# The first four output tiles, not two, in turns by halves of k, with their loads in that order

## The chip, the cores and the metric

One core of a Trainium2 chip runs the kernel. The metric is device time in microseconds (us): 407.63 is the median of three runs before the change (407.6 to 407.68).

## What is computed

Eight sequences of 256 tokens, 1024 wide. Each sequence is first multiplied by a 1024 x 1024 matrix that its expert number picks (`weight[itok]`). The result goes through a base matrix with bias and through a routed low-rank update, and is added to x:

```python
w = weight[adapter_ids]
xc = jnp.einsum('bsi,boi->bso', x, w)
...
logits = xf @ W_router.T
probs = jax.nn.softmax(logits, axis=-1)
topk_p, topk_i = jax.lax.top_k(probs, TOP_K)
...
h = jnp.einsum('nd,erd->ner', xf, A_stack) * combine[..., None]
lora_out = jnp.einsum('ner,eor->no', h, B_stack) * SCALING
out = x + xf @ W_base.T + b_base + lora_out
```

All is float32.

## The kernel before

TensorE works on operands that are split in a high part (a cast to the reduced type, ScalarE, L488 and L466) and a low part (raw minus high, VectorE, L660 and L539). A product is high x high + high x low + low x high.

The sequences go in two groups of four. For each sequence s, the first stage (`cond`) makes eight output tiles t of 128 x 256. One output tile needs one weight tile of 512 KB (w(s,t), all eight k blocks) and the sequence's x (two halves of 512 KB, four k blocks each). On TensorE it is eight wide matmuls (L801: weight high against x high and low, 512 columns), then eight narrow ones (L805: weight low against x high, 256 columns). Tile t uses PSUM bank t % 4. When a tile is done, ScalarE copies a half of the bank (L503), VectorE adds the other half to it (L686), ScalarE casts the sum (L508), VectorE subtracts (L691). TensorE may use a bank again when L686 is done (`xc_summed`). After the odd sequences the router (L844, L845) multiplies these sums: its first matmul waits until L691 has run for 15 of the 16 tiles, the last k block for the 16th. Then come the low-rank product and, after four sequences, the base matrix.

All loads of x and weights go through six raw slots of 512 KB and, but for the first x half, through SyncE's queue, in the order of `load_order`. Before a load SyncE waits until VectorE has subtracted what lay in the slot. The slot of the n-th load is n % 6, and the order of the start is the list `START`. Ahead of the first weight load of a sequence SyncE reads the expert number from memory (L357), after the wait for that load's slot.

The head is special, since nothing is there yet. The x half (0,0) is loaded in two pieces by ScalarE's queue (`ACT_MOVES`), and others in pieces by SyncE (`SP_MOVES`: tile, first and last k block). Casts and subtracts go by pieces too (`HI_PIECES`, `LO_PIECES`, in that order on ScalarE and VectorE). `START_STEPS` says in which order TensorE takes halves of output tiles: (0, 0, 4) is tile 0 with k blocks 0 to 3. The first two tiles are done so: first half of 0, first half of 1, second half of 0, second half of 1. Ahead of them run 24 matmuls on zeros (`WARM`). Below, W2a is the first half (k blocks 0 to 3) of weight tile 2 of the first sequence, W2b the second, x a and x b the halves of x.

Of the kernel before, what the change touches and what calls it, by code (L numbers as in the profile page):

```python
# [12 lines left out]
P = 128  # L13
SEQS, TOK, D = 8, 256, 1024
KT = D // P
HT = KT // 2
# [34 lines left out]
            ("A22b", R2, (1, 1)), ("A12b", R0, (0, 1))]  # L51


STARTS = 4
START = [("x", 0, 0), ("w", 0, 0), ("w", 0, 1), ("x", 0, 1), ("w", 0, 2), ("w", 0, 3)]
X0, W0, W1, X1 = range(STARTS)
ACT_MOVES = [(X0, 0, 2), (X0, 2, 4)]
SP_MOVES = [(W0, 0, 4), (W1, 0, 4), (X1, 0, 4), (W0, 4, 8), (W1, 4, 8)]
HI_PIECES = [(X0, 0, 2), (X0, 2, 4), (W0, 0, 2), (W0, 2, 4), (W1, 0, 4), (X1, 0, 2), (X1, 2, 4), (W0, 4, 8),
             (W1, 4, 8)]  # L60
LO_PIECES = [(X0, 0, 2), (X0, 2, 4), (W0, 0, 2), (W0, 2, 4), (W1, 0, 4), (X1, 0, 2), (X1, 2, 4), (W0, 4, 8),
             (W1, 4, 8)]

START_STEPS = [(0, 0, 4), (1, 0, 4), (0, 4, 8), (1, 4, 8)]
WARM, WARM_N = 24, 2 * P

RESIDENT = {(0, 5): [("a", 0, 0)], (2, 5): [("b", 0, 0)]}

# [50 lines left out]
def split_order():  # L119

    order = START[STARTS:]
    for g in range(GROUPS):
# [23 lines left out]
def load_order():  # L146

    out, n = [], 0
    for g in range(GROUPS):
        ring = list(START) if g == 0 else []  # L150
        for s in range(GSEQS * g, GSEQS * (g + 1)):
# [19 lines left out]
def piece_count(pieces, i, k):  # L171

    return next(n + 1 for n, (j, a, b) in enumerate(pieces) if j == i and a <= k < b)


def tile_steps(i):
    return KT if START[i][0] == "w" else HT

# [19 lines left out]
def build(nc, x, ids, w_cond, w_base, w_router, lora_a, lora_b, bias, consts, out):  # L198
    with ExitStack() as ctx:
# [3 lines left out]
        def psum(name):  # L203
            return ctx.enter_context(nc.psum_tensor(name, [P, 512], F32))

        def sem(name):
            return ctx.enter_context(nc.semaphore(name))
# [34 lines left out]
        bank_x = [psum(f"bank_x{m}") for m in range(HT)]  # L242
# [7 lines left out]
        raw_in = [sem(f"raw_in{i}") for i in range(RAW)]  # L250
        start_in = {(i, b): sem(f"start_in{i}_{b}") for i, a, b in ACT_MOVES + SP_MOVES if b < tile_steps(i)}
        warm_clear = sem("warm_clear")
# [54 lines left out]
        def split_dst(key, hl):  # L307
            kind, i, j = key
            if kind == "w":
                return wc_hl[:, slot_of(i, j), hl]  # L310
            if kind == "x":
                return x_hl[:, i % 2, HT * j:HT * (j + 1), hl, :]
            if kind == "S":
                return wc_hl[:, pair_of(i, j[0]) + j[1], hl]
            if kind == "T":
                return half(t_buffer(j[0]), j[1])[:, :, hl]
            if kind == "a":
                return a_hl[:, hl]
            return b_hl[:, hl, 0:KT] if kind == "b" else b_hl[:, hl, KT:]
# [12 lines left out]
        def piece(v, i, a, b):  # L332

            n = v.shape[1] // tile_steps(i)
            return v[:, a * n:b * n]

        def piece_in(i, b):
            return raw_in[i] if b == tile_steps(i) else start_in[i, b]

        def move_piece(issuer, i, a, b, src):  # L340
            issuer.dma_start(piece(raw[:, i], i, a, b), piece(src, i, a, b)).then_inc(piece_in(i, b), 16)  # L341

        def moved(i, k):

            return piece_in(i, next(b for j, a, b in ACT_MOVES + SP_MOVES if j == i and a <= k < b))

        @block.sync
        def _(sp):
            ids_of = {}

            def source(key):
                kind, i, j = key
                if kind == "x":
                    return x[i, j]
                if kind == "w":
                    if i not in ids_of:
                        ids_of[i] = nc.sync.value_load(ids[0:1, i:i + 1], min_val=0, max_val=w_cond.shape[0] - 1)  # L357
                    return w_cond[bass.ds(ids_of[i], 1), j, :, :].rearrange("a p n -> (a p) n")
                if kind in ("a", "b"):
                    return lora_a if kind == "a" else lora_b  # L360
                oh, ih = next(q for name, _, q in QUARTERS if name == kind)
                return w_base[oh, ih, :, j, :]

            def wait_free(key):
# [18 lines left out]
            for n, (key, slot) in enumerate(LOADS):
                if n >= STARTS:
                    if slot in in_slot:
# [57 lines left out]
        def _(act):  # L443
            def hi(key):
                kind, i, j = key
                if key in SUM:
                    act.wait_ge(summed, SUM[key])
                elif kind == "S":
                    name = {P1: "A11", P2: "A12", P4: "A22b"}[j[0]]
                    slot, landed = LANDED[name, i, j[1]]  # L450
                    act.wait_ge(raw_in[slot], landed)
                elif kind != "T":
                    slot, landed = LANDED[key]
                    act.wait_ge(raw_in[slot], landed)

                if kind == "S" and j[0] >= P5:
                    act.wait_ge(product_done, made(i, j[0] - 2, 2 * j[1] + 1))
                if kind == "T" and j[0] in (P6, P7, P4):
                    act.wait_ge(product_done, made(i, {P6: P1, P7: P2, P4: P5}[j[0]], HT - 1))
                if kind == "x" and i and i % GSEQS == 0:  # L460
                    act.wait_ge(product_done, made(i // GSEQS - 1, P6, HT - 1))
                if kind == "x" and i > GSEQS and i % GSEQS == 1:
                    act.wait_ge(product_done, made(i // GSEQS - 1, P7, HT - 1))
                if kind == "w" and i and i % GSEQS == 0 and j < 4:
                    act.wait_ge(product_done, made(i // GSEQS - 1, P4 if j < 2 else P3, 2 * (j % 2) + 1))
                nc.scalar.copy(split_dst(key, HI), split_src(key)).then_inc(hi_done, 1)  # L466
# [17 lines left out]
            for i, a, b in ACT_MOVES:  # L484
                move_piece(nc.scalar, i, a, b, x[START[i][1], START[i][2]])
            for i, a, b in HI_PIECES:
                act.wait_ge(moved(i, b - 1), 16)
                nc.scalar.copy(piece(split_dst(START[i], HI), i, a, b), piece(split_src(START[i]), i, a, b)) \  # L488
                    .then_inc(start_hi, 1)
            for key in START[STARTS:]:  # L490
                hi(key)
# [41 lines left out]
        def _(dve):  # L533
# [123 lines left out]

            for i, a, b in LO_PIECES:
                dve.wait_ge(start_hi, piece_count(HI_PIECES, i, b - 1))
                nc.vector.tensor_tensor(piece(split_dst(START[i], LO), i, a, b), piece(split_src(START[i]), i, a, b),  # L660
                                        piece(split_dst(START[i], HI), i, a, b).bitcast(F32), ALU.subtract) \
                    .then_inc(start_lo, 1)
            for key in START[STARTS:]:
                lo(key)
# [118 lines left out]
        def _(pe):  # L783
# [24 lines left out]
            def first_cond():  # L808

                for t, a, b in START_STEPS:  # L810
                    w, ps = (W0, W1)[t], bank_x[t]
                    for k in range(a, b):
                        pe.wait_ge(start_hi, piece_count(HI_PIECES, w, k))
                        pe.wait_ge(start_lo, piece_count(LO_PIECES, X0 if k < HT else X1, k % HT))
                        wide(ps, 0, t, k)
                    for k in range(a, b):
                        pe.wait_ge(start_lo, piece_count(LO_PIECES, w, k))
                        mm = narrow(ps, 0, t, k)
                    if b == KT:
                        mm.then_inc(cond_done, 1)  # L820
# [99 lines left out]
            for g in range(GROUPS):  # L920
                for s in range(GSEQS * g, GSEQS * (g + 1)):
                    for t in range(KT):
                        if s == 0 and t < 2:
                            if t == 0:
                                first_cond()
                            continue
                        cond(s, t)
                        if s % GSEQS == 2 and t == 1:
                            gate_to_rows(2 * g)
                    if s % 2:  # L930
                        router(s // 2)
                        lora_down(s // 2)
                second(g, P1)
                gate_to_rows(2 * g + 1)
                for j in (P2, P5, P6, P7, P4, P3):
                    second(g, j)
# [42 lines left out]
```

## Time and profile before

| | |
|---|---|
| median of three runs | 407.63 us |
| the profiled execution, its own time | 407.98 us |
| its span in the trace | 406.2 us |
| TensorE busy | 399.7 us (98%) |
| VectorE busy | 302.5 us (74%) |
| ScalarE busy | 186.3 us (46%) |
| HBM read | 64.10 MB |

The span is what the trace covers; the time of an execution has 1.8 us around it. A busy share near 100% says which engine the end depends on, not that each of its instructions is fast. All times below are us from the start of the span.

### The profile page before, as it was taken

How to read it: one execution, taken by the hardware profiler on the slowest of the kernel's cores; microseconds unless marked ns; L12 is line 12 of the kernel's file. 1: busy time of each engine (PE TensorE's matmuls, PEld its weight loads, DVE VectorE, ACT ScalarE, POOL GpSimd, SP SyncE). 2: the span in 40 equal slices, each digit the busy share in tenths (PEclk: the TensorE clock that was granted, in tenths of full speed). 3: DMA queues.
4: the chain of work that ended last, by engine and by line, in shares of the span. 5: the costliest groups of instructions: out<-in, count | busy, mean ns of one | idle time of the engine just before them, and what ended most of it. 6: DMA issues, size and time to landing. Idle time of an engine off the chain costs nothing.

```text
span 406.2 us, 5339 instructions
## 1 busy us (share of the span) xinstructions
PE 399.7 (98%) x2008; PEld 338.7 (83%) x2008; DVE 302.5 (74%) x432; ACT 186.3 (46%) x286; POOL 39.9 (10%) x67
## 2 busy tenths in 40 slices
PE   7999999999999999999999999999999999999996
PEld 6788888888888888888888888888888888888885
DVE  3888947789799999764547697478868999987322
ACT  4776834758633345221145686257666233441000
POOL 0101100101000130011162000000000003001110
PEclk9999999999999999999999999999999999999999
DMA  6999780778430056376569878146184003621222
GB/s 228 361 322 318 295 329 24 249 247 284 156 103 2 27 181 208 129 242 224 194 216 368 298 246 302 61 148 224 44 266 142 7 21 103 200 94 76 79 79 77
DMA packets 21210, 72.84 MB, mean 179 GB/s; under 512 B 2832, under 2 KB 2848, under 8 KB 21184
## 3 DMA queue, kind: packets, MB, share of 16 engines
q1 hardware_dynamic: 15984, 56.11, 40.1%
q0 software_dynamic: 4912, 15.87, 11.1%
q10 hardware_dynamic: 288, 0.52, 0.4%
q8 instruction: 16, 0.26, 0.3%
q14 instruction: 10, 0.08, 0.1%
HBM read 64.10 MB, written 8.39 MB: 178 GB/s over the span
## 4 chain that ended last, share of the span: by engine, by line
PE 96%; DMA 1%; SPq 1%; DVE 0%; issue 0%; ACT 0%
PE bank_x L801 29%; PE bank_x L805 15%; PE bank_y L786 9%; PE bank_y L787 9%; PE bank_y L788 9%; PE bank_x L786 8%; PE bank_x L787 8%; PE bank_x L788 8%; PE bank_y L844 2%; PE bank_y L845 2%; DMA raw<-w_cond 1%; PE bank_y L868 0%; SPq L357 0%; SPq L341 0%; PE bank_y L860 0%; DVE out_sb L590 0%
## 5 line engine op out<-in xcount | busy, mean ns | idle before, releaser
L801 PE MATMUL bank_x<-x_hl,wc_hl 128*128 128x512 f32 x512 | 128.8, 393 | 2.1 <-ACT wc_hl L488 2.1
L466 ACT CAST wc_hl<-raw 128x1024 fp32r<-128x1024 f32 x90 | 94.0, 1051 | 69.4 <-PE bank_y L788 34.8
L539 DVE TENSOR_TENSOR wc_hl<-raw,wc_hl 128x1024 fp32r<-128x1024 f32 x90 | 108.7, 1220 | 23.0 <-ACT wc_hl L466 22.9
L801 PEld LDWEIGHTS bank_x<-x_hl,wc_hl 128*128 128x128 f32 x512 | 92.1, 189 | 18.9 <-ACT wc_hl L488 2.5
L805 PEld LDWEIGHTS bank_x<-x_hl,wc_hl 128*128 128x128 f32 x512 | 70.1, 190 | 5.2
L805 PE MATMUL bank_x<-x_hl,wc_hl 128*128 128x256 f32 x512 | 71.7, 282 | 0.0
L582 DVE SCALAR_TENSOR_TENSOR out_sb<-bank_x,bias_sb,out_sb 128x512 f32<-128x512 f32 x32 | 23.7, 747 | 24.6 <-PE bank_x L788 19.1
L418 POOL DMA_DIRECT2D out<-out_sb x28 | 15.3, 545 | 257.7 <-DVE out_sb L590 236.1
L786 PE MATMUL bank_x<-x_hl,wc_hl 128*128 128x512 f32 x96 | 37.4, 389 | 0.0
L788 PE MATMUL bank_x<-x_hl,wc_hl 128*128 128x512 f32 x96 | 37.4, 389 | 0.0
L787 PE MATMUL bank_x<-x_hl,wc_hl 128*128 128x512 f32 x96 | 37.3, 389 | 0.0
L508 ACT CAST xc_hl<-xp 128x256 fp32r<-128x256 f32 x64 | 26.0, 406 | 24.0 <-DVE xp L686 23.8
L503 ACT COPY xc_low<-bank_x 128x256 f32<-128x256 f32 x64 | 23.7, 370 | 25.1 <-PE bank_x L805 24.9
L686 DVE TENSOR_TENSOR xp<-bank_x,xc_low 128x256 f32<-128x256 f32 x64 | 26.8, 418 | 7.7 <-ACT xc_low L503 7.4
L691 DVE TENSOR_TENSOR xc_hl<-xp,xc_hl 128x256 fp32r<-128x256 f32 x64 | 26.8, 419 | 7.6 <-ACT xc_hl L508 7.6
L590 DVE TENSOR_TENSOR out_sb<-bank_y,out_sb 128x512 f32<-128x512 f32 x24 | 16.4, 688 | 18.6 <-PE bank_y L788 17.8
L412 POOL DMA_DIRECT2D out_sb<-x x32 | 22.7, 714 | 76.2 <-PE bank_x L805 76.0
L786 PE MATMUL bank_y<-xc_hl,wc_hl 128*128 128x512 f32 x64 | 25.0, 390 | 0.0
L787 PE MATMUL bank_y<-xc_hl,wc_hl 128*128 128x512 f32 x64 | 24.9, 389 | 0.0
L788 PE MATMUL bank_y<-xc_hl,wc_hl 128*128 128x512 f32 x64 | 24.9, 389 | 0.0
L466 ACT CAST x_hl<-xp 128x1024 fp32r<-128x1024 f32 x16 | 16.6, 1051 | 13.8 <-DVE xp L543 13.5
L786 PEld LDWEIGHTS bank_x<-x_hl,wc_hl 128*128 128x128 f32 x96 | 18.0, 188 | 3.8
(94 smaller groups left out, 507.7 us busy)
## 6 DMA issues: line engine op xcount, KB each, us to landing
raw<-w_cond SPq DMA_DIRECT2D x62, 512.0 KB, 5.3
raw<-w_base SPq DMA_DIRECT2D x24, 512.0 KB, 5.0
out_sb<-x POOLq DMA_DIRECT2D x32, 256.0 KB, 5.5
raw<-x SPq DMA_DIRECT2D x15, 512.0 KB, 5.1
out<-out_sb POOLq DMA_DIRECT2D x28, 256.0 KB, 2.3
raw<-w_cond SPq DMA_DIRECT2D x4, 256.0 KB, 4.8
out<-out_sb SPq DMA_DIRECT2D x4, 256.0 KB, 2.0
raw<-x ACTq DMA_DIRECT2D x2, 256.0 KB, 2.8
```

The costliest lines, as they stand in the source:

```text
L466: nc.scalar.copy(split_dst(key, HI), split_src(key)).then_inc(hi_done, 1)
L503: nc.scalar.copy(xc_low[:, t % 2], bank_x[t % HT][:, TOK:]).then_inc(low_copied, 1)
L508: nc.scalar.copy(xc_hl[:, t, HI, s % 2 * TOK:(s % 2 + 1) * TOK], xp[:, s // 2 % 2, t, s % 2 * TOK:(s % 2 + 1) * TOK]).then_inc(xc_hi, 1)
L539: nc.vector.tensor_tensor(split_dst(key, LO), split_src(key), split_dst(key, HI).bitcast(F32), ALU.subtract).then_inc(lo_done, 1)
L582: nc.vector.scalar_tensor_tensor(out_sb[:, o], bank_x[m][:], bias_sb[:, i:i + 1], out_sb[:, o], ALU.add, ALU.add).then_inc(pass_done, 1)
L686: nc.vector.tensor_tensor(xc, bank_x[t % HT][:, 0:TOK], xc_low[:, t % 2], ALU.add) \
L691: nc.vector.tensor_tensor(xc_hl[:, t, LO, s % 2 * TOK:(s % 2 + 1) * TOK], xc, xc_hl[:, t, HI, s % 2 * TOK:(s % 2 + 1) * TOK].bitcast(F32), ...
L786: nc.tensor.matmul(ps, w_hi, v_hi, start=start, stop=False, skip_group_check=resumed)
L787: nc.tensor.matmul(ps, w_hi, v_lo, start=False, stop=False, skip_group_check=resumed)
L788: return nc.tensor.matmul(ps, w_lo, v_hi, start=False, stop=stop, skip_group_check=resumed)
L801: nc.tensor.matmul(ps[:], wc_hl[:, slot_of(s, t), HI, k], x_hl[:, s % 2, k].rearrange("p h n -> p (h n)"), start=(k == 0), stop=False)
L805: return nc.tensor.matmul(ps[:, TOK:], wc_hl[:, slot_of(s, t), LO, k], x_hl[:, s % 2, k, HI], start=False, stop=(k == KT - 1))
```

## The change

The first four output tiles are taken in turns: first halves of 0, 1, 2, 3, then second halves of 0, 1, 2, 3. The loads are put in the order of use: x a, W0a, W1a, W2a, x b, W3a, W0b, W1b, W2b, W3b. Formerly x b came after W1a, and W2 and W3 were each one load of 512 KB, behind W1b. W0a is loaded in two pieces of 128 KB. The places of x b and W2 in the six slots are exchanged. One warm matmul of 24 is left out.

```diff
-STARTS = 4
-START = [("x", 0, 0), ("w", 0, 0), ("w", 0, 1), ("x", 0, 1), ("w", 0, 2), ("w", 0, 3)]
-X0, W0, W1, X1 = range(STARTS)
+STARTS = 6
+START = [("x", 0, 0), ("w", 0, 0), ("w", 0, 1), ("w", 0, 2), ("x", 0, 1), ("w", 0, 3)]
+X0, W0, W1, W2, X1, W3 = range(STARTS)
 ACT_MOVES = [(X0, 0, 2), (X0, 2, 4)]
-SP_MOVES = [(W0, 0, 4), (W1, 0, 4), (X1, 0, 4), (W0, 4, 8), (W1, 4, 8)]
-HI_PIECES = [(X0, 0, 2), (X0, 2, 4), (W0, 0, 2), (W0, 2, 4), (W1, 0, 4), (X1, 0, 2), (X1, 2, 4), (W0, 4, 8),
-             (W1, 4, 8)]
...
+SP_MOVES = [(W0, 0, 2), (W0, 2, 4), (W1, 0, 4), (W2, 0, 4), (X1, 0, 4), (W3, 0, 4), (W0, 4, 8), (W1, 4, 8),
+            (W2, 4, 8), (W3, 4, 8)]
+HI_PIECES = [(X0, 0, 2), (X0, 2, 4), (W0, 0, 2), (W0, 2, 4), (W1, 0, 4), (W2, 0, 4), (X1, 0, 2), (X1, 2, 4),
+             (W3, 0, 4), (W0, 4, 8), (W1, 4, 8), (W2, 4, 8), (W3, 4, 8)]
+LO_PIECES = HI_PIECES
+
+START_STEPS = [(t, a, a + HT) for a in (0, HT) for t in range(4)]
+WARM, WARM_N = 23, 2 * P
...
-                    w, ps = (W0, W1)[t], bank_x[t]
+                    w, ps = (W0, W1, W2, W3)[t], bank_x[t]
...
-                        if s == 0 and t < 2:
+                        if s == 0 and t < 4:
```

On ScalarE, from its first casts of the start on (the names in brackets are semaphores: start_in1_2 is the load of the first two k blocks of start tile 1, raw_in4 the last load into slot 4):

```order
-L488 CAST wc_hl<-raw 128x256 [waits start_in1_4] x2
+L488 CAST wc_hl<-raw 128x256 [waits start_in1_2]
+L488 CAST wc_hl<-raw 128x256 [waits start_in1_4]
 L488 CAST wc_hl<-raw 128x512 [waits start_in2_4]
-L488 CAST x_hl<-raw 128x2x256 [waits raw_in3] x2
+L488 CAST wc_hl<-raw 128x512 [waits start_in3_4]
+L488 CAST x_hl<-raw 128x2x256 [waits raw_in4] x2
+L488 CAST wc_hl<-raw 128x512 [waits start_in5_4]
 L488 CAST wc_hl<-raw 128x512 [waits raw_in1]
 L488 CAST wc_hl<-raw 128x512 [waits raw_in2]
-L466 CAST wc_hl<-raw 128x1024 [waits raw_in4]
-L466 CAST wc_hl<-raw 128x1024 [waits raw_in5]
```

The cast of W2a now stands ahead of the two casts of x b and that of W3a right behind them; the whole tiles W2 and W3 are gone from behind W1b, and their second halves take their place.

On SyncE's queue, at the loads of the second half of the start (those on L341 wait for nothing, the next on L387 are the first that wait for a slot):

```order
 L341 DMA raw<-w_cond 128x512
-L387 ISA
-L387 DMA raw<-w_cond 128x1024
-L387 ISA
-L387 DMA raw<-w_cond 128x1024
+L341 ISA
+L341 DMA raw<-w_cond 128x512
+L341 ISA
+L341 DMA raw<-w_cond 128x512
+L341 ISA
+L341 DMA raw<-w_cond 128x512
 L387 ISA [waits start_lo]
 L387 DMA raw<-w_cond 128x1024
```

Two loads of whole weight tiles have become loads of halves, so ten loads, not seven, go out on SyncE before the first that waits for a slot.

## Rows read from the trace of the kernel before

**Rows 1.** Page: busy time per engine; granted clock in slices.

```profile
PE 399.7 (98%) x2008; PEld 338.7 (83%) x2008; DVE 302.5 (74%) x432; ACT 186.3 (46%) x286; POOL 39.9 (10%) x67
...
PEclk9999999999999999999999999999999999999999
```

**Rows 2.** Waits of TensorE, 0 to 110 us: total, times, longest.

```profile
PE bank_x L801 <- ACT wc_hl L488: 2.1, 2, 1.5
```

**Rows 3.** Timeline of TensorE: start us, duration us, what, [idle before].

```profile
6.50 1.19 PE L801 MATMUL bank_x<-x_hl,wc_hl 128*128 128x512 f32 x4 [0.56 <-ACT wc_hl L488]
...
11.06 1.19 PE L801 MATMUL bank_x<-x_hl,wc_hl 128*128 128x512 f32 x4 [1.50 <-ACT wc_hl L488]
...
12.57 1.09 PE L801 MATMUL bank_x<-x_hl,wc_hl 128*128 128x512 f32 x4
...
13.97 2.02 PE L801 MATMUL bank_x<-x_hl,wc_hl 128*128 128x512 f32 x8
...
19.57 0.63 PE L801 MATMUL bank_x<-x_hl,wc_hl 128*128 128x512 f32 x2
```

**Rows 4.** Timeline of ScalarE, 2 to 16 us.

```profile
6.05 0.71 ACT L488 CAST wc_hl<-raw 128x256 fp32r<-128x256 f32 x2 [1.35 <-DMA raw<-w_cond]
...
8.95 1.14 ACT L488 CAST x_hl<-raw 128x512 fp32r<-128x512 f32 x2 [1.35 <-DMA raw<-x]
10.39 0.62 ACT L488 CAST wc_hl<-raw 128x512 fp32r<-128x512 f32 x1 [0.31 <-DMA raw<-w_cond]
11.30 0.62 ACT L488 CAST wc_hl<-raw 128x512 fp32r<-128x512 f32 x1 [0.28 <-DMA raw<-w_cond]
12.78 1.05 ACT L466 CAST wc_hl<-raw 128x1024 fp32r<-128x1024 f32 x1 [0.86 <-DMA raw<-w_cond]
14.02 1.05 ACT L466 CAST wc_hl<-raw 128x1024 fp32r<-128x1024 f32 x1 [0.20 <-DMA raw<-w_cond]
```

**Rows 5.** All waits of ScalarE, 14.5 to 50.4 us.

```profile
ACT xc_hl L508 <- DVE xp L686: 5.0, 8, 1.4
ACT wc_hl L466 <- DMA raw<-w_cond: 2.4, 3, 1.5
ACT a_hl L466 <- DMA raw<-lora_a: 0.2, 1, 0.2
```

**Rows 6.** Timeline of all engines ahead of the router.

```profile
48.77 1.05 ACT L466 CAST wc_hl<-raw 128x1024 fp32r<-128x1024 f32 x1 [0.69 <-DMA raw<-w_cond]
...
50.50 0.37 ACT L503 COPY xc_low<-bank_x 128x256 f32<-128x256 f32 x1 [0.37 <-PE bank_x L805]
...
52.23 0.42 DVE L691 TENSOR_TENSOR xc_hl<-xp,xc_hl 128x256 fp32r<-128x256 f32 x1 [0.47 <-ACT xc_hl L508]
52.98 0.19 PEld L844 LDWEIGHTS bank_y<-xc_hl,wr_hl 128*128 128x128 f32 x1
```

**Rows 7.** Timeline of ScalarE near 28 us.

```profile
27.94 1.05 ACT L466 CAST wc_hl<-raw 128x1024 fp32r<-128x1024 f32 x1 [1.54 <-DMA raw<-w_cond]
```

**Rows 8.** Timeline of SyncE's queue: issues of loads.

```profile
2.79 0.94 SPq L341 DMA_DIRECT2D raw<-w_cond  x2
...
21.02 1.30 SPq L387 DMA_DIRECT2D raw<-w_cond  x2
```

**Rows 9.** Timeline of VectorE: subtract of weight tile 4, ahead of SyncE's expert read.

```profile
16.59 1.22 DVE L539 TENSOR_TENSOR wc_hl<-raw,wc_hl 128x1024 fp32r<-128x1024 f32 x1
```

**Rows 10.** Line L357, 0 to 60 us: ns min/median/max, first and last start.

```profile
L357 SPq TENSOR_LOAD <-ids_ptr x3: 837/1357/2169, 0.7 to 39.5; - x3
```

**Rows 11.** DMA in 2.4:3.2, in 4:6 and in 28:33 us.

```profile
DMA packets 161, 0.30 MB, mean 371 GB/s; under 512 B 16, under 2 KB 16, under 8 KB 161
...
DMA packets 257, 0.49 MB, mean 243 GB/s; under 512 B 25, under 2 KB 25, under 8 KB 257
...
DMA packets 559, 2.03 MB, mean 406 GB/s; under 512 B 64, under 2 KB 64, under 8 KB 559
```

**Rows 12.** Windows: length, busy per engine, clock, DMA share, GB/s.

```profile
21.50:22.00 0.50, 0.50 (x6) 0.50 (x5) 0.50 (x1) 0.50 (x3) 0.00 (x0) 1.00 0.41 81
```

More of the change, by code:

```diff
@@ L51 @@
             ("A22b", R2, (1, 1)), ("A12b", R0, (0, 1))]
-STARTS = 4
-START = [("x", 0, 0), ("w", 0, 0), ("w", 0, 1), ("x", 0, 1), ("w", 0, 2), ("w", 0, 3)]
-X0, W0, W1, X1 = range(STARTS)
+STARTS = 6
+START = [("x", 0, 0), ("w", 0, 0), ("w", 0, 1), ("w", 0, 2), ("x", 0, 1), ("w", 0, 3)]
+X0, W0, W1, W2, X1, W3 = range(STARTS)
 ACT_MOVES = [(X0, 0, 2), (X0, 2, 4)]
-SP_MOVES = [(W0, 0, 4), (W1, 0, 4), (X1, 0, 4), (W0, 4, 8), (W1, 4, 8)]
-HI_PIECES = [(X0, 0, 2), (X0, 2, 4), (W0, 0, 2), (W0, 2, 4), (W1, 0, 4), (X1, 0, 2), (X1, 2, 4), (W0, 4, 8),
-             (W1, 4, 8)]
[L61 to L65, printed above, removed]
+SP_MOVES = [(W0, 0, 2), (W0, 2, 4), (W1, 0, 4), (W2, 0, 4), (X1, 0, 4), (W3, 0, 4), (W0, 4, 8), (W1, 4, 8),
[5 more added lines that the diff above has]
+WARM, WARM_N = 23, 2 * P
 RESIDENT = {(0, 5): [("a", 0, 0)], (2, 5): [("b", 0, 0)]}
```

## The prediction

> **What bounds the kernel now.** I read the page's first lines, then the chain of waits, then the timelines of the first 20 us, then everything up to 56 us on the engines that feed TensorE. TensorE is busy for 399.7 of 406.2 us at granted clock 1.00 in all stretches read [rows 1], so the end moves only if TensorE idles less. Up to 110 us TensorE waits for data in two places, 2.1 us together, both for a cast of ScalarE on line L488 [rows 2]. The timeline of TensorE shows them [rows 3]: 0.56 us before the first product at 6.50, and 1.50 us before 11.06. A half-step (four wide and four narrow matmuls of one output tile) takes 12.57 - 11.06 = 1.51 us right after a stall and 13.97 - 12.57 = 1.40 us else. From 11.06 six half-steps' worth follow without a gap, until output tile 4 starts at 19.57, 8.51 us later.
>
> Why does it stall at 11.06? ScalarE is itself idle, waiting for DMA, before almost every cast [rows 4]: the second half of x could be cast at 8.95, the second half of weight tile 0 (W0b below; a and b are halves of k) at 10.39. Its cast takes 0.62, and TensorE starts at 11.06. So the head of the kernel is bound by bytes arriving. The order of arrival, in KB summed from the first piece of x on, was: 1536 at 8.95, 1792 at 10.39, 2048 at 11.30, 2560 at 12.78, 3072 at 14.02.
>
> **A second bound, behind the first.** Between 14.5 and 50.4 us ScalarE never waits for TensorE: its waits are for VectorE and for DMA alone [rows 5]. It copies the banks and casts the next tiles late, always after TensorE has long finished. So in that stretch the chain SyncE -> DMA -> ScalarE -> VectorE runs in its own time and does not get faster when TensorE does. It meets TensorE again at the router: its first matmul (L844) starts its weight load at 52.98, and needs the low part of the 15th output tile, which VectorE ends at 52.23 + 0.42 = 52.65 [rows 6]. With 0.04 us for the hand-over (cast end 11.02 to start 11.06 in [rows 3, 4]) the slack is 52.98 - 52.69 = **0.29 us**. Backwards, that subtract stands on VectorE behind the subtract of a weight tile whose cast, at 48.77, ended an idle of 0.69 for a DMA [rows 6]. What set this chain's pace earlier is again a DMA: 1.54 us of idle before the cast at 27.94 [rows 7]. Those loads went out from SyncE at 21.02 and later [rows 8], after SyncE had waited for weight tile 4's low part (16.59 + 1.22 = 17.81, [rows 9]) and then read the second sequence's expert number; 21.02 - 17.81 = 3.2 us.
>
> **The change, part by part.**
>
> *One warm matmul less.* The warm matmuls are followed by an idle 0.56 [rows 3] and nothing waits for their end: 0. TensorE's clock is granted in full in every slice, the one with the 1.50 us stall too [rows 1], so I expect nothing from that side.
>
> *W0a in two loads of 128 KB.* The first cast now needs half the bytes. Before, 256 KB issued at 2.79 could be cast at 6.05. At the 371 GB/s that the x pieces reached [rows 11] 128 KB take 0.35, so the first product may start about 0.3 earlier. But this gains nothing at the end if TensorE stalls for bytes again afterwards, and it will (next item). Its cost: one more issue on SyncE ahead of all others. Two issues take 0.94 us [rows 8], so one half a microsecond, and the DMA engines were not full then: 243 GB/s between 4 and 6 us [rows 11]. Everything behind may come 0 to 0.5 us later; I take 0.15, near the low end: an issue takes half a microsecond while its 256 or 512 KB take 0.7 or 1.4 at 371 GB/s, so a backlog forms behind the first loads and a late issue vanishes in it.
>
> *Four tiles by halves, loads in that order.* TensorE now has three half-steps (W0a, W1a, W2a) on the first x half where it had two. The matmuls are the same in number and shape. W2a's 256 KB go ahead of the second x half, so that half lands 256 KB later. Now the fourth half-step, W3a. It needs W3a cast, and in ScalarE's order that stands behind the casts of x's second half. W3a is complete when 2048 KB are in, exactly the place of W1b before: 11.30. Plus cast 0.62, hand-over 0.04, and the 0.15 above: TensorE can start it at about 12.1. ScalarE is free by then (x's 512 KB, done at 1792 KB = 10.4, two casts 1.14, end 11.5). Meanwhile TensorE: the first two half-steps began at 6.50 and ended at 11.06 - 1.50 = 9.56 before; 0.3 earlier and with W2a's 1.40 behind them they end at 10.7: **it stalls for about 1.4 us again**, in place of 1.50. After it five half-steps remain to tile 4, not six: 8.51 - 1.40 = 7.11. Tile 4 starts at 12.1 + 7.11 = 19.2 instead of 19.57: **gain 0.36**, between 0.0 (all half a microsecond late) and 0.5 (nothing late). Each later half comes in time: W0b would be cast at 12.7 for 13.6, W1b at 13.5 for 15.0, W3b (3072 KB, 14.02) at 14.8 for 17.8. VectorE has halves to subtract where it had two whole tiles, and can begin each as soon as its cast is done, so W3b's low part should be there near 15.5.
>
> *Tile 4 and the slots.* Raw slots of W0 and W1 are freed later, by the later landing of W0b and W1b (1.3 us each: 512 KB of others now go first), so the loads of weight tiles 5 and 6 go out near 13.4 and 14.1. The DMA queue may run dry near 14.5 for half a microsecond. It ran dry at 21.5 anyway (81 GB/s [rows 12]), because SyncE sat in the expert read, so that is taken back before the loads at 21.02. Cost 0, and 0.5 if that cover fails. Weight tile 4 itself lands at the same sum of bytes. Its subtract can begin at 16.4 to 17.0 (before 16.59): the second chain moves by D = -0.2 to +0.4; I take 0.
>
> *Sum.* The router can start 0.29 - D earlier and TensorE arrives 0.36 earlier; the smaller counts. Gain 0.29. Against the profile's own time: 407.98 - 0.29 = 407.69; the median of the runs is 0.35 below that execution, so **407.3**. Behind the router TensorE bounds again (ScalarE waits for it from 50.5 on, [rows 6]), and the gain stays.
>
> **A rule against the change.** The smallest loads in sight, 2 KB rows, ran at 371 GB/s, the 4 KB rows at 406 [rows 11]. By these, the 1 MB of W2 and W3 that now goes in 2 KB rows costs 1049 / 371 - 1049 / 406 = 0.24 us more (1049 thousand bytes); that is inside D. By the row the time is 407.3 to 407.6. The Trainium skill ("DMA: Bandwidth & Descriptors", section "Bandwidth") asks to batch loads to 1 MiB or more for three quarters of the peak, and would count every cut as a loss; its section on small descriptors knows only about three cycles of overhead per packet, which is closer to this row. By the first of the two the time would be that of the second rival, by the other the forecast.
>
> **The rivals.**
> 1. *Forecast*: stall moved, not removed; router caps the gain. 407.1 to 407.6. Chance 0.60.
> 2. *Smaller loads slow the bytes.* W0b and W1b, 256 KB each, came 0.91 apart; W2 and W3, 512 KB each, 1.24 apart [rows 4]. If the size makes the difference, four halves take 3.64 where two whole tiles took 2.48: weight tile 4 is 1.16 later, the expert read and all behind it as well, D = 1.1, and TensorE waits 1.1 - 0.29 = 0.8 at the router: **408.4**. It ends slower than before as soon as D is above 0.29. For it: those intervals. Against: 371 GB/s in [rows 11]. (The Trainium skill's rule on batching, above, would lead here.) Chance 0.2, and most of it part-way, 407.7 to 408.4.
> 3. *The stall goes and the chain moves too.* If W3a arrived by 10.7, TensorE would gain 1.8; still 0.29 - D is the cap, so the chain must be faster. The expert's read could be: its first part took between 0.84 and 2.17 us in the three reads up to 60 us [rows 10]. With D = -0.4 to -0.8 the gain is 0.7 to 1.1, the time 406.5 to 406.9. Against: nothing makes the bytes come sooner. Chance 0.08.
> 4. *The change does nothing*: the earlier issues cost 0.5 and W3a starts at 12.45. 407.6 to 407.8. Chance 0.12.
>
> **How the numbers follow.** 407.3 is the first case. A measurement of this kernel can tell about 0.2%, 0.8 us. Faster by more needs case 3 at its end: 0.05. Slower by more needs case 2 at its full price or a little over: 0.06. The range 406.8 to 408.1 leaves out the far ends of cases 2 and 3, some 1 in 10.
>
> **What the changed profile would show.** Right: TensorE idle 1.2 to 1.5 us before a group near 12.1 with L488 as the releaser, tile 4 near 19.2, no ScalarE wait for TensorE until about 50, and a new small idle, or none, before L844 near 52.7. Wrong: a wait at the router of half a microsecond (case 2; the loads of the second sequence issued after 21.5), or no stall near 11 and the router at 51. The prediction breaks if a load behind slot order, such as tile 5's, comes after 20.9: TensorE wants it at 19.2 + 2.8 = 22.0, and its cast takes 1.05 [rows 4].

## The result and the profile after

The changed kernel takes 409.11 us (median of 14 runs) against 407.99 us of the kernel before beside it: ratio 1.0026, interval 1.0015 to 1.0038. It was measured three times in all, each time beside the kernel before; its median was 1.12, 0.69 and 0.38 us above that kernel's, on average **0.73 us** (resampled over all runs: 0.49 to 1.08). Forecast was 407.3, that is 0.3 faster than the 407.63 on record. Of the 1.8 us between 407.3 and 409.11, 0.36 is no effect of the change: the kernel before itself took 407.99 beside it, not 407.63. The single runs of this first measurement spread over 2 us, from 407.76 to 409.87. The profiled execution took 408.6 us. One slow execution of e2 below, at 1030 us, is left out of its median.

The page of the changed kernel, to be held against [rows 1]:

```profile
span 406.8 us, 5366 instructions
...
PE 400.5 (98%) x2007; PEld 339.1 (83%) x2007; DVE 302.8 (74%) x434; ACT 186.4 (46%) x288; POOL 40.0 (10%) x67
...
PEclk9999999999999999999999999999999999999999
```

TensorE is busy 0.8 us longer at the same clock, and the span is 0.6 longer. The timeline of TensorE at the head (columns as in [rows 3]):

```profile
6.24 1.08 PE L801 MATMUL bank_x<-x_hl,wc_hl 128*128 128x512 f32 x4
...
7.72 1.20 PE L801 MATMUL bank_x<-x_hl,wc_hl 128*128 128x512 f32 x4
...
9.69 1.19 PE L801 MATMUL bank_x<-x_hl,wc_hl 128*128 128x512 f32 x4 [0.31 <-ACT wc_hl L488]
...
11.98 1.18 PE L801 MATMUL bank_x<-x_hl,wc_hl 128*128 128x512 f32 x4 [0.64 <-ACT wc_hl L488]
...
19.08 2.00 PE L801 MATMUL bank_x<-x_hl,wc_hl 128*128 128x512 f32 x8
```

The first product starts at 6.24, 0.26 earlier; the cast of its two k blocks was done at 5.50 + 0.76 / 2 = 5.88 (the two casts at 5.50 took 0.76 us), and TensorE comes to it straight from the warm matmuls, without an idle. W3a starts at 11.98 after an idle of 0.64, and tile 4 at 19.08 instead of 19.57. So far this is the forecast (12.1 and 19.2); of the 1.4 us of stall that it foresaw, 0.64 stand before W3a and 0.31 before W2a, and the half-steps between took longer (9.69 - 7.72 - 0.31 = 1.66, 11.98 - 9.69 - 0.64 = 1.65). The loss comes at the end of the second sequence. Who TensorE waited for (whole execution; total, times, longest), to be held against [rows 2]:

```profile
PE bank_x L801 <- ACT wc_hl L488: 0.9, 2, 0.6
PE bank_y L844 <- DVE xc_hl L691: 0.9, 1, 0.9
```

```profile
53.08 0.43 DVE L691 TENSOR_TENSOR xc_hl<-xp,xc_hl 128x256 fp32r<-128x256 f32 x1 [0.47 <-ACT xc_hl L508]
53.62 0.19 PEld L844 LDWEIGHTS bank_y<-xc_hl,wr_hl 128*128 128x128 f32 x1 [1.07 <-issue]
53.65 0.47 PE L844 MATMUL bank_y<-xc_hl,wr_hl 128*128 128x512 f32 x1 [0.89 <-DVE xc_hl L691]
```

The low part of the 15th tile ends at 53.08 + 0.43 = 53.51, not at 52.65 as in [rows 6], and the router's first weight load goes at 53.62 instead of 52.98. That is +0.64, and the span grew by 406.8 - 406.2 = 0.6. In the profiles quoted here the span is this moment plus 353.2: 52.98 and 406.2 before, 53.62 and 406.8 after. So nothing behind the router changed the time.

Where does the second chain lose its time? The chain that ended last, in order of time (start, duration):

```profile
13.61 1.38 DVE wc_hl L660 x2
...
15.01 7.68 DMA raw<-x
...
22.72 1.06 ACT x_hl L466
...
23.80 1.23 DVE x_hl L539
...
53.08 0.44 DVE xc_hl L691
...
53.65 0.47 PE bank_y L844
```

Between 23.80 and 53.08 all of its pieces are VectorE's and ScalarE's. In this profile it hangs on the load of the second sequence's first x half: issued at 15.01, landed at 22.69. Before, it was issued at 13.18:

```profile
13.18 0.43 SPq L387 DMA_DIRECT2D raw<-x  x1
```

After, with the five last loads of the start (L341) first, and in the last row the first weight loads of the second sequence, which went out at 21.02 before [rows 8]:

```profile
5.46 2.81 SPq L341 DMA_DIRECT2D raw<-w_cond  x5
...
15.01 0.34 SPq L387 DMA_DIRECT2D raw<-x  x1
...
22.04 0.85 SPq L387 DMA_DIRECT2D raw<-w_cond  x2
```

ScalarE, after, shows the same (compare [rows 4]; the cast of that x half was at 20.18 before):

```profile
12.21 2.71 ACT L488 CAST wc_hl<-raw 128x512 fp32r<-128x512 f32 x4 [0.28 <-DMA raw<-w_cond]
...
18.30 1.05 ACT L466 CAST wc_hl<-raw 128x1024 fp32r<-128x1024 f32 x1 [1.13 <-DMA raw<-w_cond]
...
22.72 1.05 ACT L466 CAST x_hl<-raw 128x1024 fp32r<-128x1024 f32 x1 [1.52 <-DMA raw<-x]
```

It is idle for 1.13 and 1.52 us waiting for tile 5 and for that x half. What VectorE loses by it is in the windows (length, then busy time of PE, PEld, DVE, ACT and POOL with their counts, clock, DMA share, GB/s). Before:

```profile
8.00:10.00 2.00, 1.56 (x10) 1.18 (x8) 0.72 (x2) 1.05 (x2) 0.00 (x0) 1.00 0.95 308
10.00:12.00 2.00, 0.94 (x4) 0.80 (x5) 1.63 (x4) 1.32 (x3) 0.00 (x0) 1.00 1.02 400
...
14.00:23.00 9.00, 9.00 (x53) 7.91 (x52) 8.98 (x13) 8.15 (x13) 1.74 (x3) 1.00 0.90 332
23.00:32.00 9.00, 9.00 (x52) 7.87 (x52) 7.87 (x12) 5.83 (x10) 0.71 (x1) 1.00 0.98 353
32.00:37.00 5.00, 5.00 (x31) 4.45 (x30) 3.00 (x6) 3.40 (x8) 0.20 (x1) 1.00 0.96 333
```

After:

```profile
8.00:10.00 2.00, 1.69 (x9) 1.30 (x9) 0.73 (x2) 0.62 (x1) 0.00 (x0) 1.00 0.84 232
10.00:12.00 2.00, 1.36 (x9) 1.00 (x7) 1.43 (x3) 1.66 (x3) 0.00 (x0) 1.00 0.86 251
...
14.00:23.00 9.00, 9.00 (x52) 7.87 (x51) 6.95 (x11) 5.85 (x11) 1.75 (x3) 1.00 0.87 318
23.00:32.00 9.00, 9.00 (x52) 7.88 (x51) 8.20 (x12) 8.13 (x14) 0.71 (x1) 1.00 0.95 343
32.00:37.00 5.00, 5.00 (x31) 4.41 (x30) 3.53 (x7) 2.19 (x5) 0.70 (x1) 1.00 0.96 348
```

Two things are to be seen. VectorE was busy 8.98 of 9.00 us between 14 and 23, and is now for 6.95. Of the 2.03 us lost it has caught up 0.33 + 0.53 = 0.86 by 37. The rest is 1.17; at the router it is late by 0.86, so some 0.3 more were caught up behind 37. It could catch up because in the kernel before it had an idle of its own behind 23, for the cast of a weight tile of the second sequence:

```profile
29.02 1.23 DVE L539 TENSOR_TENSOR wc_hl<-raw,wc_hl 128x1024 fp32r<-128x1024 f32 x1 [1.07 <-ACT wc_hl L466]
```

And between 8 and 12 us the DMA engines moved 2 x (308 + 400) = 1416 KB before and 2 x (232 + 251) = 966 KB after. The change promised to use the bytes better; it gets fewer of them.

### The profile page after: what moved, and what is told of

It reads as the page before. It is cut to its first block, busy times and chain, and to the rows that moved or that the text cites. A ratio compares the mean times of both kernels' runs of the same rounds, so it can differ in the third digit from the quotient of the medians.

```text
span 406.8 us, 5366 instructions
## 1 busy us (share of the span) xinstructions
PE 400.5 (98%) x2007; PEld 339.1 (83%) x2007; DVE 302.8 (74%) x434; ACT 186.4 (46%) x288; POOL 40.0 (10%) x67
## 4 chain that ended last, share of the span: by engine, by line
PE 86%; DVE 7%; DMA 3%; SPq 1%; ACT 1%; issue 0%
PE bank_x L801 22%; PE bank_x L805 11%; PE bank_y L786 9%; PE bank_y L788 9%; PE bank_y L787 9%; PE bank_x L786 8%; PE bank_x L788 8%; PE bank_x L787 8%; DVE wc_hl L539 3%; DMA raw<-x 2%; PE bank_y L844 2%; PE bank_y L845 2%; DMA raw<-w_cond 2%; DVE x_hl L539 1%; DVE xp L686 1%; DVE xc_hl L691 1%
## 5 line engine op out<-in xcount | busy, mean ns | idle before, releaser
L466 ACT CAST wc_hl<-raw 128x1024 fp32r<-128x1024 f32 x88 | 91.9, 1051 | 67.8 <-PE bank_y L788 34.8
L539 DVE TENSOR_TENSOR wc_hl<-raw,wc_hl 128x1024 fp32r<-128x1024 f32 x88 | 106.4, 1221 | 22.2 <-ACT wc_hl L466 22.2
L590 DVE TENSOR_TENSOR out_sb<-bank_y,out_sb 128x512 f32<-128x512 f32 x24 | 16.4, 689 | 18.6 <-PE bank_y L788 17.8
```

Of the source, the lines that this page charges most:

```text
L539: nc.vector.tensor_tensor(split_dst(key, LO), split_src(key), split_dst(key, HI).bitcast(F32), ALU.subtract).then_inc(lo_done, 1)
```

## The experiments

All differences are to the kernel before measured beside it, median against median, in us. Single runs scatter by about 1 us either way, so one difference is good to 0.3 or 0.4; the profiles say more on the mechanism than the times.

**e1 and g3, the changed kernel again.**

> The changed kernel once more, unaltered, beside the others. About 1.0 us over the kernel before. The router's first matmul waits 0.5 to 1.2 us for VectorE; TensorE starts output tile 4 near 19.1.

> The changed kernel unaltered, a third time: 0.6 to 1.1 us over the kernel before; 240 to 260 GB/s between 10 and 12 us.

+0.69 (ratio 1.0015, 1.0003 to 1.0028) and +0.38 (1.0008, 0.9996 to 1.0020). Both are slower than the kernel before, as expected, but by less than the 1.0 and the 0.6 to 1.1 expected. In the three profiles (the result's, e1's, g3's) TensorE started tile 4 at 19.08, 19.58 and 19.40 and waited 0.9, 0.4 and 1.3 us for VectorE at the router. The x half of the next sequence was issued at 15.01, 15.73 and 15.77 and cast at 22.72, 21.98 and 23.51. So the wait is there each time. But the x half alone does not set its size: in e1 it was cast 0.74 us earlier than in the first profile, and VectorE was as late at the router (0.82 against 0.86 us). There another load held the chain behind it, that of the low-rank matrix, which SyncE issued at 23.92, right behind the second sequence's first two weight loads (23.02; 21.02 before):

```profile
30.42 1.05 ACT L466 CAST a_hl<-raw 128x1024 fp32r<-128x1024 f32 x1 [1.33 <-DMA raw<-lora_a]
```

These loads stand behind SyncE's read of the expert number. In the three profiles they went out at 22.04, 23.02 and 22.95. Tile 4's low part, for which the read waits, ended at 17.86, 18.56 and 18.57 (17.81 before), and from there to the issue it took 4.2, 4.5 and 4.4 us (3.2 before).

**e4, small loads alone.**

```diff
-SP_MOVES = [(W0, 0, 4), (W1, 0, 4), (X1, 0, 4), (W0, 4, 8), (W1, 4, 8)]
+SP_MOVES = [(W0, 0, 4), (W1, 0, 4), (X1, 0, 4), (W0, 4, 8), (W1, 4, 8), (W2, 0, 4), (W2, 4, 8), (W3, 0, 4),
+            (W3, 4, 8)]
...
+START_STEPS = [(0, 0, 4), (1, 0, 4), (0, 4, 8), (1, 4, 8), (2, 0, 8), (3, 0, 8)]
```

> The kernel before with W2 and W3 each loaded, cast and subtracted in two halves; order of loads, slots and TensorE's work as before. Theory B: W3 is complete about 1.0 us later than 14.0, the chain behind moves by that, and the time rises by 0.5 to 0.9 us. Theory A: loads of tiles 5 and 6 still go out early, so the bytes keep coming; W3 at most 0.2 us later, time within 0.2 us of the kernel before.

+0.02 (0.9991, 0.9978 to 1.0003). ScalarE casts four halves of weight tiles without a gap between them; the second row is the second sequence's first x half:

```profile
12.48 2.61 ACT L488 CAST wc_hl<-raw 128x512 fp32r<-128x512 f32 x4 [0.37 <-DMA raw<-w_cond]
...
20.27 1.06 ACT L466 CAST x_hl<-raw 128x1024 fp32r<-128x1024 f32 x1
```

The x half is cast at 20.27, as before (20.18). That is what the expectation had for theory A. The second rival of the prediction, that 256 KB loads of these tiles move fewer bytes, is out (0.5 to 0.9 us of loss were expected for it), and with it the batching rule of the Trainium skill ("DMA: Bandwidth & Descriptors", section "Bandwidth") as an account of this loss.

**e2, the old slots.** The rows of START in the old order, so that x b has slot 3 again and W2 slot 4; loads and work as in the changed kernel.

```diff
-START = [("x", 0, 0), ("w", 0, 0), ("w", 0, 1), ("w", 0, 2), ("x", 0, 1), ("w", 0, 3)]
-X0, W0, W1, W2, X1, W3 = range(STARTS)
+START = [("x", 0, 0), ("w", 0, 0), ("w", 0, 1), ("x", 0, 1), ("w", 0, 2), ("w", 0, 3)]
+X0, W0, W1, X1, W2, W3 = range(STARTS)
```

> The changed kernel with the old assignment of slots (x b in slot 3, W2 in slot 4), so that the load of the next sequence's first x half waits for x b's low part and not for W2b's. Theory A (slots come free too late, DMA runs dry near 15 us): that load goes out 0.4 us earlier than 15.0, and the chain gains 0.3 to 0.5 us, the time falls by as much against the changed kernel. Theory B (256 KB loads move fewer bytes per us): the bytes are late in any case, no change within 0.2 us.

+0.91 (1.0017, 1.0004 to 1.0030). The load went out at 15.06, no earlier: in SyncE's queue it stands behind the loads of tiles 5 and 6, and they wait for W0b and W1b. This edit could not test what it was meant to test.

**e3, the expert numbers read early.**

```diff
                 in_slot[slot] = key
+                if key == ("w", 0, 4):
+                    for i in (1, 2):
+                        ids_of[i] = nc.sync.value_load(ids[0:1, i:i + 1], min_val=0, max_val=w_cond.shape[0] - 1)
```

> The changed kernel with the expert numbers of sequences 1 and 2 read right after the issue of weight tile 4, while SyncE waits for a slot anyway. If the chain SyncE, DMA, ScalarE, VectorE is what holds the router (both theories A and B agree), the second sequence's first weight load goes out at about 18 instead of 22.0 us, the wait at the router shrinks, and the time falls by 0.9 us or more, to at least 0.3 us under the kernel before. If the router waits for something else, nothing changes.

+0.76 (1.0010, 0.9996 to 1.0025), the forecast of this run was a miss. Its waits and its issues:

```profile
PE bank_x L804 <- ACT wc_hl L491: 1.7, 1, 1.7
PE bank_y L921 <- DVE warm L537: 1.2, 1, 1.2
```

```profile
15.96 0.34 SPq L387 DMA_DIRECT2D raw<-x  x1
...
18.93 2.30 SPq L387 DMA_DIRECT2D raw<-w_cond  x2
```

The second sequence's first weight load went out at 18.93 instead of 22.04, and in this profile the router did not wait; but TensorE had a 1.7 us stall at W3a and came late itself (tile 4 at 19.61). The low part of the 15th tile:

```profile
52.32 0.43 DVE L694 TENSOR_TENSOR xc_hl<-xp,xc_hl 128x256 fp32r<-128x256 f32 x1 [0.47 <-ACT xc_hl L511]
```

It ended at 52.75, only 0.10 later than in the kernel before, although the x half was cast as late as 21.92. So in this one profile the second chain made up for its late loads once the weights behind them came sooner. The time shows no use of it; whether it would help without the stall, this run does not tell.

**f1, x b in slot 1.** x b is the first tile to be used up whole, so its slot goes to the load of tile 5.

```diff
-START = [("x", 0, 0), ("w", 0, 0), ("w", 0, 1), ("w", 0, 2), ("x", 0, 1), ("w", 0, 3)]
-X0, W0, W1, W2, X1, W3 = range(STARTS)
+START = [("x", 0, 0), ("x", 0, 1), ("w", 0, 0), ("w", 0, 1), ("w", 0, 2), ("w", 0, 3)]
+X0, X1, W0, W1, W2, W3 = range(STARTS)
```

> The changed kernel with the raw slots handed out so that x b has slot 1 and W0, W1, W2, W3 have slots 2 to 5: x b is used up first, so the load of weight tile 5 can go out at about 12 us, not 13.6, and each further load one place sooner. Theory A (the loads behind the start go out too late because the slots come free too late): the gap in the DMA near 15 us closes, the cast of the second sequence's first x half moves from 22 to 22.7 us back to 20.2 to 21, the wait at the router falls to 0.2 or less, and the time falls by 0.4 to 0.8 us against the changed kernel. Theory B2 (the bytes of the start themselves come late): the x half's cast stays later than 21.5 and the time within 0.2 us.

+0.26 (1.0003, 0.9993 to 1.0013), 0.47 less than the changed kernel's average (about as much as the error; 0.4 to 0.8 were expected). In the profile tile 5's load went out at 12.47 (13.73 in the changed kernel, 11.90 before). The x half still went out only at 15.54 and was cast at 21.83, later than the 20.2 to 21 expected, because W0b came late in this execution (cast at 13.51 after 1.28 us of waiting for the DMA).

**f2, f1 with e3's early read.**

> The same with the expert numbers of sequences 1 and 2 read early. With both delays of the second chain gone, TensorE should not wait at the router at all, and the time is the kernel before's less what tile 4 starts earlier than 19.57: 0.1 to 0.5 us under the kernel before.

+0.36 (1.0006, 0.9990 to 1.0021): not better than f1, a miss of the forecast once more. But the edit has a price of its own. The two reads stand in SyncE's queue ahead of tile 5's load. x b's low part, which frees that load's slot, ended at 11.97; the reads ran from 8.4 to 14.7, and the load went out at 14.88, where it was 12.47 in f1. The reads by line, then SyncE's issues from 14 us on:

```profile
L391 SPq TENSOR_LOAD <-ids_ptr x2: 837/2172/3506, 8.4 to 12.8; - x2
...
14.88 0.85 SPq L387 DMA_DIRECT2D raw<-w_cond  x2
```

In f4 below it was the same (slot free at 13.11, load at 14.74). So f2 and f4 do not show that the late read is harmless; in e3 the slot itself came free only at 14.55, and the reads delayed nothing.

**f3 and g2, W0a whole.**

```diff
-SP_MOVES = [(W0, 0, 2), (W0, 2, 4), (W1, 0, 4), (W2, 0, 4), (X1, 0, 4), (W3, 0, 4), (W0, 4, 8), (W1, 4, 8),
+SP_MOVES = [(W0, 0, 4), (W1, 0, 4), (W2, 0, 4), (X1, 0, 4), (W3, 0, 4), (W0, 4, 8), (W1, 4, 8),
```

> The changed kernel with W0a loaded whole (256 KB) as before. If the extra issue and the 1 KB rows of the split cost the start its bytes, W3a's cast and all after it come 0.2 to 0.5 us earlier, tile 4 starts before 19.1 and the time falls by 0.3 us. If they cost nothing, TensorE's first product is about 0.3 us later and the rest as in the changed kernel.

> The changed kernel with W0a whole, a second time, beside the changed kernel itself. Theory S: 0.4 to 1.0 us faster than the changed kernel in the same call. Theory A: no difference beyond 0.3 us.

0.00 (1.0005, 0.9995 to 1.0016) and +0.29 (1.0013, 1.0001 to 1.0025); together +0.14, which is 0.59 under the changed kernel, but 0.09 under it where the two stood side by side (g2 and g3), against 0.4 to 1.0 expected. TensorE started tile 4 at 18.99 and 18.84. Between 10 and 12 us these profiles had 316 and 364 GB/s, the three of the changed kernel 251, 255 and 250.

**g1, the split alone, in the kernel before.**

```diff
-SP_MOVES = [(W0, 0, 4), (W1, 0, 4), (X1, 0, 4), (W0, 4, 8), (W1, 4, 8)]
+SP_MOVES = [(W0, 0, 2), (W0, 2, 4), (W1, 0, 4), (X1, 0, 4), (W0, 4, 8), (W1, 4, 8)]
```

> The kernel before with one edit alone: W0a in two loads of 128 KB. Theory S (the split costs the start its bytes): fewer GB/s between 8 and 12 us than before's 308 and 400, W0b's cast 0.3 us or more later than 10.39, tile 4 later than 19.57, time 0.3 to 0.8 us over the kernel before. Theory A (slots alone): nothing, or the first product 0.3 us earlier; time within 0.2 us.

-0.11 (0.9999, 0.9990 to 1.0008), and 399 GB/s between 10 and 12 us. In the old order the split costs nothing that the times can show. Its one profile did have tile 4 at 20.07 and the router at 53.47, each 0.5 later than before, but that execution took 408.49, the longest of its eleven.

**i1, both mends.** f1's slots and f3's whole W0a.

> The changed kernel with both mends: W0a whole and x b in raw slot 1. If the two causes add up, the time is 0.2 to 0.5 us under the kernel before (the changed kernel is 0.8 over it, each mend takes 0.5 to 0.6 away). If they are one cause, it is no better than either, 0.1 to 0.3 us over the kernel before.

-0.41 (0.9989, 0.9980 to 0.9999), within the 0.2 to 0.5 expected if the two add up; they do. Tile 5's load went out at 11.69, the x half was cast at 20.19, as early as before, tile 4 started at 18.86, and the router, which did not wait, at 52.27.

**f4, W3a ahead of x b.** f2 with the first halves of all four tiles ahead of x b, in the loads and in the casts and subtracts.

```diff
-SP_MOVES = [(W0, 0, 2), (W0, 2, 4), (W1, 0, 4), (W2, 0, 4), (X1, 0, 4), (W3, 0, 4), (W0, 4, 8), (W1, 4, 8),
+SP_MOVES = [(W0, 0, 2), (W0, 2, 4), (W1, 0, 4), (W2, 0, 4), (W3, 0, 4), (X1, 0, 4), (W0, 4, 8), (W1, 4, 8),
...
-HI_PIECES = [(X0, 0, 2), (X0, 2, 4), (W0, 0, 2), (W0, 2, 4), (W1, 0, 4), (W2, 0, 4), (X1, 0, 2), (X1, 2, 4),
-             (W3, 0, 4), (W0, 4, 8), (W1, 4, 8), (W2, 4, 8), (W3, 4, 8)]
+HI_PIECES = [(X0, 0, 2), (X0, 2, 4), (W0, 0, 2), (W0, 2, 4), (W1, 0, 4), (W2, 0, 4), (W3, 0, 4), (X1, 0, 2),
+             (X1, 2, 4), (W0, 4, 8), (W1, 4, 8), (W2, 4, 8), (W3, 4, 8)]
```

> As f2, with W3a loaded, cast and subtracted ahead of x b: all four first halves of TensorE's work run on x a. They end near 12.0; x b is complete with 2048 KB, near 11.3 to 11.6, so the second halves start near 12.9: tile 4 at about 18.6, 1.0 us earlier than before. With the second chain freed the time is 0.6 to 1.0 us under the kernel before.

+0.08 (1.0000, 0.9988 to 1.0011). Tile 4 started at 18.82, but the router waited 0.6 us. A miss by 0.7 us.

**g4, h3 and i2, f4 with W0a whole and without the early read.** Against the changed kernel it has f1's slots, f3's whole W0a and f4's order.

```diff
-SP_MOVES = [(W0, 0, 2), (W0, 2, 4), (W1, 0, 4), (W2, 0, 4), (W3, 0, 4), (X1, 0, 4), (W0, 4, 8), (W1, 4, 8),
+SP_MOVES = [(W0, 0, 4), (W1, 0, 4), (W2, 0, 4), (W3, 0, 4), (X1, 0, 4), (W0, 4, 8), (W1, 4, 8),
```

> All four first halves on x a (W3a ahead of x b), W0a whole, x b in raw slot 1. TensorE could be at tile 4 near 18.6. If VectorE's chain is what holds the router, most of that is lost there: the router starts at 52.1 to 52.4, the time is 0.3 to 0.7 us under the kernel before. If not, the time is 0.9 us under it.

> g4 unaltered: 0.6 to 1.1 us under the kernel before, tile 4 between 17.9 and 18.4.

> g4 unaltered, for the third time: 0.3 to 0.9 us under the kernel before, as g4 and h3 were in their calls.

-0.87 (0.9980, 0.9968 to 0.9993), -0.25 (0.9986, 0.9971 to 1.0000), -0.36 (0.9989, 0.9976 to 1.0002): on average **-0.49** (-0.79 to -0.22), faster than both kernels. The third is within its expectation, the second gained less than the 0.6 to 1.1 expected. For the first, 0.3 to 0.7 and a router at 52.1 to 52.4 were expected if VectorE's chain holds it; it started at 51.46, since that chain itself had come earlier, as the rows show. The first of the three profiles, TensorE at the head and the router:

```profile
9.63 1.09 PE L801 MATMUL bank_x<-x_hl,wc_hl 128*128 128x512 f32 x4
...
11.03 1.09 PE L801 MATMUL bank_x<-x_hl,wc_hl 128*128 128x512 f32 x4
...
12.43 1.09 PE L801 MATMUL bank_x<-x_hl,wc_hl 128*128 128x512 f32 x4
...
18.05 2.02 PE L801 MATMUL bank_x<-x_hl,wc_hl 128*128 128x512 f32 x8
```

```profile
50.56 0.43 DVE L691 TENSOR_TENSOR xc_hl<-xp,xc_hl 128x256 fp32r<-128x256 f32 x1 [0.47 <-ACT xc_hl L508]
...
51.46 0.19 PEld L844 LDWEIGHTS bank_y<-xc_hl,wr_hl 128*128 128x128 f32 x1
```

No stall from W2a (9.63) on. All four half-steps run on x a while x b arrives, tile 4 starts at 18.05, and VectorE is ready (50.99) before TensorE needs it (51.46). This was the good case: in the other two tile 4 started at 18.44 and 19.13, and the router at 51.84 and 52.71. i1, with x b ahead of W3a as in the changed kernel, is as fast within the error, so the place of W3a is not shown to matter.

**h1, h2 and h4: what costs the bytes?** h1 is g4 with the split of W0a, h2 with a split of W1a instead (its casts and subtracts too), h4 with the 4 KB load of the bias moved from GpSimd's queue to SyncE's, behind W0a.

h1 and h2, SyncE's loads (g4's line, then each of theirs), and h4:

```diff
-SP_MOVES = [(W0, 0, 4), (W1, 0, 4), (W2, 0, 4), (W3, 0, 4), (X1, 0, 4), (W0, 4, 8), (W1, 4, 8),
+SP_MOVES = [(W0, 0, 2), (W0, 2, 4), (W1, 0, 4), (W2, 0, 4), (W3, 0, 4), (X1, 0, 4), (W0, 4, 8), (W1, 4, 8),
...
+SP_MOVES = [(W0, 0, 4), (W1, 0, 2), (W1, 2, 4), (W2, 0, 4), (W3, 0, 4), (X1, 0, 4), (W0, 4, 8), (W1, 4, 8),
...
+                if (i, a) == (W0, 0):
+                    nc.sync.dma_start(bias_sb[:], bias).then_inc(bias_in, 16)
```

> g4 with W0a in two loads of 128 KB again. If the split costs this order its bytes: GB/s between 8 and 12 us fall from 350 and 339 to below 300, tile 4 starts 0.5 us or more after 18.05, and the time rises by 0.5 to 1.0 us over g4's. If not, the time is within 0.3 us of g4's, and the difference between f4 and g4 came from the early read of the expert numbers.

> g4 with W1a, not W0a, in two loads of 128 KB (and its cast and subtract in two). One issue and 128 KB loads as in h1, but behind W0a. If an additional issue or short rows anywhere in the start cost bytes, as slow as h1; if only what stands first in the queue matters, like g4.

> g4 with the 4 KB load of the bias moved from GpSimd's queue to SyncE's, right behind W0a: one issue more at the place where the split puts one, but no short rows of weights. If the delay of the issues costs the bytes, 0.4 us or more slower than g4; if the short rows do, within 0.3 us of it.

+0.14, +0.35 and +0.23 (ratios 0.9998, 1.0002, 0.9999, each with an interval of about 0.0014 either way), where g4 beside them (h3) had -0.25: 0.4 to 0.6 slower than g4, all three. h1 was expected 0.5 to 1.0 slower, h4 0.4 or more. Windows of g4, h1 and h4:

```profile
8.00:10.00 2.00, 2.00 (x14) 1.78 (x13) 1.56 (x3) 1.04 (x2) 0.00 (x0) 1.00 0.98 350
10.00:12.00 2.00, 2.00 (x13) 1.69 (x12) 1.28 (x3) 1.58 (x3) 0.00 (x0) 1.00 0.98 339
```

```profile
8.00:10.00 2.00, 2.00 (x13) 1.74 (x13) 1.28 (x2) 0.91 (x2) 0.00 (x0) 1.00 1.02 315
10.00:12.00 2.00, 2.00 (x13) 1.74 (x12) 0.95 (x2) 1.18 (x3) 0.00 (x0) 1.00 0.95 274
```

```profile
8.00:10.00 2.00, 1.38 (x9) 1.04 (x7) 0.24 (x2) 0.69 (x2) 0.00 (x0) 1.00 0.90 300
10.00:12.00 2.00, 2.00 (x11) 1.74 (x12) 1.40 (x3) 1.32 (x3) 0.00 (x0) 1.00 0.94 299
```

These three move fewer bytes than this g4 (2 x 689 = 1378 KB against 1178 and 1198 in h1 and h4; h2 had 1142), also h4, which adds 4 KB and no short rows of weights. But the other two profiles of g4 had 1350 and 1202 KB, so the bytes alone do not separate them. Each difference in time, too, is within its error; that all three, f3, g2 and i1 point the same way makes it likely, not certain, that one more issue near the head of SyncE's queue costs about half a microsecond in these orders of the loads; in the old order (g1) it did not.

## Why the prediction was wrong

**What held.** The picture of two chains was right. The stall was moved, not removed: forecast 12.1 for W3a, measured 11.98, 12.47 and 12.30; the gain to tile 4, forecast 0.36, was 0.49, -0.01 and 0.17. The router caps it, as [rows 5, 6] had it, and TensorE's wait there appeared in all three profiles. The 0.29 us of slack fits: 53.51 - 52.65 = 0.86 late, less 0.29, and 0.07 more for the hand-over after a real wait, give 0.64, the growth of the span (the hand-over is 53.62 - 53.51 = 0.11 now, where 0.04 was assumed).

**The step that failed** is "Tile 4 and the slots": its "Cost 0, and 0.5 if that cover fails", and with it D, of which the text took 0 and at most 0.4. D at the router was 0.86, 0.82 and 1.59 in the three profiles, more than the slack in each. The text knew that the slots of W0 and W1 come free later (forecast 13.4 for tile 5's load, measured 13.73, 14.54 and 14.54, before 11.90) and that the DMA queue would run dry. It held that SyncE's read of the expert number gives this back before the loads at 21.02. Two things were wrong with that.

- The tiles 5, 6 and the x half are used before those loads, and VectorE was busy 8.98 of 9.00 us there, so it could not take up what came late. It caught up part of it behind 23 us, not all.
- The cover was not there either. The loads of 21.02 went out at 22.04, 23.02 and 22.95, since the read took 4.2 to 4.5 us instead of 3.2 and, in two of the profiles, began 0.75 later. The prediction had named this itself as a sign of being wrong ("the loads of the second sequence issued after 21.5").

D was also read at the wrong place. The text took it from tile 4's subtract, forecast 16.4 to 17.0; that began at 16.63, 17.34 and 17.35. In the first profile it moved by 0.04 only, and D at the router was 0.86 all the same: most of it arose behind tile 4. How much of D comes from the late slots, how much from the late read and how much from the split (next paragraph) is not settled. In e3's profile, with the numbers read early, D was 0.10, but its time is no better than the changed kernel's, and f2's early reads held up tile 5's load.

**The second cause**, of about the same size, was also put at too little. "One more issue" was taken at 0.15: 0.4 to 0.6 us by h1, h2, h4 and by f3 and g2 together; h4 has no short rows, so these are not needed for it. It was seen only with the new orders, not in g1. For the slots, f1 against the changed kernel and i1 against f3 and g2 give 0.47 and 0.55. Both together, from +0.73 to -0.41 in i1, are more than the whole loss. So i1 shows the sum; each part alone is hardly larger than its error, and how the sum divides is not shown.

**Right by luck.** W3a's start came out as forecast, but not the stall: 0.64 us, not 1.4, stood before it, because TensorE had already lost time before W2a and in longer half-steps. And "nothing waits for their end" did not hold for the warm matmuls: with W0a there earlier, the first product (6.24) came 0.36 behind its cast (5.88), straight from the warm matmuls. At the end this cost nothing, since TensorE stalled for bytes behind it.

**The rivals.** The second named the right number (408.4, and 407.63 + 0.73 = 408.4) and the right place, the router, but a wrong reason: e4 excludes that W2 and W3 in halves are slow. Even 408.4 lies above the range's upper end, 408.1. The right rival would have been its D with other causes: the slots, the read and the split. What the prediction says of the section on small descriptors, that it knows only the three cycles per packet, is too short: the Trainium skill ("DMA: Bandwidth & Descriptors", section "Why small descriptors are slow (HBM only)") names besides them 32 bytes of descriptor metadata for each DMA operation. No run here shows either.

**Open.** Why the changed kernel's profiles show so few bytes until 12 us, when all ten loads have been issued by 5.46 + 2.81 = 8.3, is not settled; nor why the read of the expert number took a microsecond longer, nor why the split did nothing in the old order (g1). The scatter of 2 us between executions of one kernel fits the arrival of the loads (W3a's start varies by 0.5 in three profiles, the x half's cast by 1.5), which was seen in profiles only, not for each run.

## What to carry to other kernels

Before counting a gain on the bound engine, find the next place where it meets the feeding chain, take the slack there as the cap, and then ask which engine of the feeding chain has no idle time where the loads will come late: only an idle that it has behind them, ahead of the meeting point, can return the loss (here 2.03 us came down to 0.86, and the slack was 0.29). Check that what is counted on as cover stays where it was. When loads are reordered, look at which slot each one frees and who waits for it in the queue; give the slot that comes free first to the next load. At the head of a kernel one more issue may cost more than the smaller first piece brings. And when an experiment moves an instruction forward in a queue, look at what now stands behind it (f2).

## What the runs showed of the hardware

Between 10 and 12 us the changed kernel's DMA engines were 86% busy and moved 251 GB/s, those of the kernel before 102% and 400. Over the busy share this is 251 / 0.86 = 292 against 392 GB/s: busy engines are not full engines, and the share of busy time hid a quarter of the rate. The Trainium skill ("Perfetto Trace Analysis", section "Identifying the Most-Contended Engine") calls the occupancy of the 16 DMA engines misleading; these windows agree. One more load near the head of SyncE's queue, of 4 KB (h4) as of 128 (h1), went with 0.4 to 0.6 us more at the end, though its issue takes only half a microsecond and the queue had gone ahead of the DMA; in the old order (g1) it went with none.

Reading an expert number on SyncE in the midst of its loads took 3.2 us from the end of the wait to the next issue in the kernel before, and 4.2, 4.5 and 4.4 us in the changed one. Two such reads placed earlier ran from 8.4 to 14.7 us in f2, and a load whose slot was free at 11.97 went out at 14.88.
